# The second cross attention's keys and folded query weights computed at the end of the routed stage before it

## The reference, cut to what matters

```
x = x + tanh(g_ffn[0])   * L0_ffn(layernorm(x))        # 8 experts, top 2 of them for each token
x = x + tanh(g_xattn[1]) * L1_xattn(layernorm(x), ctx, ctx, mask, W_Q, W_K, W_V, W_O)

L1_xattn: Q = x W_Q, K = ctx W_K, V = ctx W_V (16 heads of 64)
          softmax(mask(Q K^T / 8)) V W_O
```

## Time and profile before

| | |
|---|---|
| median of 3 runs | 1459.25 us (1458.04 to 1459.87) |
| the profiled execution: its own time | 1460.75 us |
| its span, first to last instruction | 1458.9 us |
| mean granted TensorE clock | 0.862 of full |
| PE / PEld busy | 1148.7 us (79%) / 793.9 us (54%) |
| DVE / ACT / POOL busy | 708.8 us (49%) / 614.8 us (42%) / 442.1 us (30%) |
| L0f's loop ends on PE | 399.3 us after the span's start |
| L1 opens | 419.1 us |
| L1's first scores | 452.2 us |

### The profile page before, as it was taken

The page is one execution under the profiler, slowest core; times in us unless marked ns, Lnnn a source line. Parts: engine busy times, 40 slices in busy tenths (PEclk is TensorE's granted clock), DMA queues, the critical chain, the costliest instruction groups (busy, mean ns, idle before and its releaser), DMA issues. The chain is left out here.

```text
span 1458.9 us, 26569 instructions
## 1 busy us (share of the span) xinstructions
PE 1148.7 (79%) x8750; PEld 793.9 (54%) x8750; DVE 708.8 (49%) x3304; ACT 614.8 (42%) x1531; POOL 442.1 (30%) x636
## 2 busy tenths in 40 slices
PE   5997875399959999989997874998476999962594
PEld 3675744287725566654444764787352444442473
DVE  3564547133337777634452444111755788755012
ACT  3453442133247776624213230333362666630353
POOL 1673514423403644510000416344010000015343
PEclk8998987599979999999997875699785999975797
DMA  7599120222079940011620011465234222040343
GB/s 198 135 265 226 37 102 28 68 75 83 16 117 120 161 77 2 1 33 44 150 58 15 2 59 41 122 173 137 60 114 126 67 54 68 20 138 18 85 133 91
DMA packets 150263, 128.36 MB, mean 88 GB/s; under 512 B 13205, under 2 KB 126796, under 8 KB 150137
## 3 DMA queue, kind: packets, MB, share of 16 engines
q1 hardware_dynamic: 135256, 107.65, 31.5%
q0 software_dynamic: 7824, 15.32, 4.0%
q10 hardware_dynamic: 7056, 3.81, 1.0%
HBM read 88.89 MB, written 40.85 MB: 89 GB/s over the span
## 5 line engine op out<-in xcount | busy, mean ns | idle before, releaser
L306 POOL TENSOR_TENSOR L_Z<-L_Z,L_mx 128x512 f32<-128x512 f32 x84 | 88.5, 1055 | 276.9 <-DVE L_mx L617 276.9
L2991 DVE CUSTOM_DVE_ANT_0 L3s_masked<-L3s_psS,L3s_trilw 128x512 f32<-128x512 f32 (+3 forms) x256 | 109.0, 487 | 34.8 <-PE L3s_psS L2890 34.3
L908 ACT ACTIVATE L_Z<-L_Z,L_nmx 128x154 f32<-128x154 f32 x256 | 105.1, 414 | 42.3 <-DVE L_nmx L965 42.2
L2962 ACT ACTIVATE L3s_E<-L3s_psT 128x512 f32<-128x512 f32 (+1 forms) x192 | 87.8, 531 | 48.8 <-PE L3s_psT L2903 48.6
L740 POOL TENSOR_TENSOR L_Z<-L_Z,L_rin 128x488 f32<-128x488 f32 x64 | 64.0, 1000 | 125.0 <-DVE L_rin L973 125.0
L617 DVE CUSTOM_DVE_ANT_0 L_Z<-L_psS,L_Z 128x154 f32<-128x154 f32 x256 | 63.4, 313 | 61.1 <-PE L_psS L354 53.6
L808 PE MATMUL L_psS<-L_G,L_xnT 128*128 128x462 f32 x192 | 82.5, 526 | 2.8 <-DVE L_nmx L965 1.4
L965 DVE CUSTOM_DVE_ANT_0 L_Z<-L_psS,L_mask 128x154 f32<-128x154 f32 x256 | 67.7, 313 | 11.4 <-PE L_psS L808 10.9
L515 ACT ACTIVATE L_E<-L_psT 128x512 f32<-128x512 f32 x84 | 46.3, 596 | 56.8 <-PE L_psT L367 56.8
L2890 PE MATMUL L3s_psS<-L3s_KS,L3s_QS 72*128 72x512 bf16 (+3 forms) x256 | 55.3, 333 | 13.0 <-PEq L2876 10.1
L983 DVE COPY L_PT<-L_psT 122x512 f32<-122x512 f32 x64 | 43.6, 682 | 40.5 <-PE L_psT L818 39.7
(11 more groups left out here) (544 smaller groups left out, 2880.7 us busy)
## 6 DMA issues: line engine op xcount, KB each, us to landing
L_Z<-in_fside_Bx16xSxS SPq DMA_DIRECT2D x16, 1232.0 KB
L2f_w<-in_L_ffn_W SPq DMA_DIRECT2D x39, 256.0 KB
slotsL<-empty SPq DMA_DIRECT2D x1, 8320.5 KB, 75.1
L1m_cb<-comb_rows SPq DMA_DIRECT2D x8, 1024.0 KB
L3f_w<-in_L_ffn_fc_w SPq DMA_DIRECT2D x32, 256.0 KB
L0f_w<-in_L_ffn_W SPq DMA_DIRECT2D x24, 256.0 KB
q_parts<-L3s_parts SPq DMA_DIRECT2D x12, 384.0 KB, 5.2
L3s_QS<-q_parts SPq DMA_DIRECT2D x16, 288.0 KB
```

What stands on the lines that cost most here:

```text
L306: nc.gpsimd.tensor_tensor(Z[:, t % NZ, h, 0:KM_], Z[:, t % NZ, h, 0:KM_], top.broadcast_to([P, HG, KM_]), ALU.subtract).then_inc(z_ready, 1)
L908: last = nc.scalar.activation(Z[:, t % 2, h], Z[:, t % 2, h], ACT.Exp, scale=-1.0, bias=nmx[:, t % 2, h:h + 1], accum_out=sums[:, t % 2, h ...
L2962: nc.scalar.activation(E[:, g.par, h, EO[group[0]]:EO[group[0]] + wd], psT[:, k, 0:wd], ACT.Exp).then_inc(t_free, 1)
L2991: last = nc.vector.tensor_tensor_reduce(masked[:, k, at:at + wd], psS[:, k, at:at + wd], trilw[:, S - wd:S], 1.0, LOW, ALU.add, ALU.max, m ...
```

## The change

A new class `Keys1` owns G, which is now allocated around both stages. `Lead0`'s four large tiles are slices of G's memory (`lend`). The keys and G are made at the end of L0f, two heads (one block j) at a time: K^T of a block goes through the two banks of `psT` into a double-buffered KT, its eight products with W_Q through `psA` (a = 0) and `psB` (a = 1) into G. PE does so right after its loop. ACT handles blocks 0 to 3 before its wait for `returned` and the issue of its reads, and one of blocks 4 to 7 ahead of each group that it scales; DVE handles blocks 0 to 3 before its additions, and one of blocks 4 to 7 ahead of each group. L1 loses the keys, the folded weights and their waits and begins with the values.

```diff
 def wide_attention(nc, m, c):
-        G = sb("G", [P, B, H, S2])
+        G = c["G"]
         @block.tensor
-            for j in range(KB): ...   # keys, L749 to L755
             for b in range(B):
                 for j in range(2):
                     n = 2 * b + j
-                    if n < 4:
-                        pe.wait_ge(k_done, 13 + n)
-                    else:
+                    if n >= 4:
                         pe.wait_ge(v_out, n - 3)
             pe.wait_ge(v_out, 2 * B)
-            pe.wait_ge(k_done, 2 * KB)
-            for b in range(B): ...    # folded weights, L774 to L787
             pe.wait_ge(r_out, B)
-            pe.wait_ge(g_out0, G3 * B)
-            pe.wait_ge(g_out1, G3 * B)
         @block.scalar    (L874 to L877 and L884 to L890 removed)
         @block.vector    (L945 to L951 removed)

 class Lead0:
-        self.w1, self.w2, self.b1 = sb("f1", [P, 4 * P]), sb("f2", [P, 4, D]), sb("fb", [P, 4])
-        self.h, self.tmp = sb("fh", [P, 2, 4, 512]), sb("tmp", [P, TB, D])
+        lend = c["keys"].lend
+        self.w1, self.w2, self.b1 = lend([P, 4 * P]), lend([P, 4, D]), sb("fb", [P, 4])
+        self.h, self.tmp = lend([P, 2, 4, 512]), lend([P, TB, D])

+class Keys1:
+    def tensor(self, pe):
+        ctx_all = self.m.ctxT[:].rearrange("p b k -> p (b k)")
+        def keys(j):
+            if j >= 1:
+                pe.wait_ge(self.k_done, 2 * j)
+            for f in range(2):
+                pe.matmul(self.psT[:, f, 0:2 * S2], self.wk[:, j * P:(j + 1) * P], ctx_all[:, f * 2 * S2:(f + 1) * 2 * S2],
+                          start=True, stop=True).then_inc(self.k_full, 1)
+        def scores_weights(j):
+            pe.wait_ge(self.k_done, 2 * j + 2)
+            if j >= 1:
+                pe.wait_ge(self.g_done0, 2 * j)
+                pe.wait_ge(self.g_done1, 2 * j)
+            for f in range(2):
+                for b in range(2):
+                    for a in range(2):
+                        at = (2 * f + b) * S2
+                        last = pe.matmul(self.banks[a][:, f, b * S2:(b + 1) * S2], self.wq[64 * a:64 * a + 64, j],
+                                         self.KT[64 * a:64 * a + 64, j % 2, at:at + S2], start=(b == 0), stop=(b == 1),
+                                         skip_group_check=True)
+                last.then_inc(self.g_full, 1)
+        keys(0)
+        for j in range(self.KB):
+            if j + 1 < self.KB:
+                keys(j + 1)
+            scores_weights(j)
+
+    def scalar(self, act, j):
+        def keep_keys(j):
+            if j >= 2:
+                act.wait_ge(self.g_full, 2 * (j - 1))
+            for f in range(2):
+                act.wait_ge(self.k_full, 2 * j + f + 1)
+                nc.scalar.mul(self.KT[:, j % 2, f * 2 * S2:(f + 1) * 2 * S2], self.psT[:, f, 0:2 * S2], self.SIGN).then_inc(self.k_done, 1)
+        if j == 0:
+            keep_keys(0)
+        if j + 1 < self.KB:
+            keep_keys(j + 1)
+        for f in range(2):
+            act.wait_ge(self.g_full, 2 * j + f + 1)
+            nc.scalar.copy(self.G[:, 2 * f:2 * f + 2, 2 * j], self.banks[0][:, f, 0:2 * S2]...).then_inc(self.g_done0, 1)
+
+    def vector(self, dve, j):     # the same for banks[1], g_done1

 class Collect:
-    def second(self, act):
+    def second(self, act, keys=None):
+        if keys is not None:
+            for j in range(TB):
+                keys.scalar(act, j)
+        for p in range(2):
+            act.wait_ge(self.m.returned[p], 16 * self.m.back[p])
         for g in range(TB):
             act.dma_start(m.XT3[:, g * TB:(g + 1) * TB], self.rows(1, g)).then_inc(self.in1[g], 16)
         act.wait_ge(self.shared, 1)
         for g in range(TB):
+            if keys is not None:
+                keys.scalar(act, TB + g)
             act.wait_ge(self.in1[g], 16)
             ...
-    def add(self, dve):
+    def add(self, dve, keys=None):
         dve.wait_ge(self.shared, 1)
+        if keys is not None:
+            for j in range(TB):
+                keys.vector(dve, j)
         for g in range(TB):
+            if keys is not None:
+                keys.vector(dve, TB + g)
             ...
```

More of the change, by code:

```diff
@@ L748, in _ @@
         def _(pe):
[L749 to L755, removed]
             for b in range(B):
@@ L873, in _ @@
         def _(act):
[L874 to L877, removed]
             act.wait_ge(var_ready, 1)
@@ L883, in _ @@
                 nc.scalar.copy(V[0:KM, b, j * 512:(j + 1) * 512], kv_bank[n % 4][0:KM, :]).then_inc(v_out, 1)
[L884 to L889, removed]
-                                   g_bank[n % 2][:, 0, 0:w * S2].rearrange("p (j k) -> p j k", k=S2)).then_inc(g_out0, 1)
             def turned_x(u):
@@ L1541, in sync @@
     def sync(self, sp):
[L1542 to L1543 removed]
+        for dst, src in ((self.w1, self.c["w1"]), (self.b1[:], self.c["b1"]), (self.w2, self.c["w2"])):
+            sp.dma_start(dst, src).then_inc(self.f_in, 16)
     def gpsimd(self, pool):
@@ L1928, in routed_experts @@
 def routed_experts(nc, m, name, c):
+    keys = c.get("keys")
     J, U, chunks = c["w1"].shape[2] // P, c["U"], c["chunks"]
@@ L1972, in routed_experts @@
         route = lead.route
+        if keys is not None:
+            keys.open(sb, sem, psT, (psA, psB))
         collect = Collect(nc, sem, m, c["key"], route.shared, c.get("out"))
@@ L2043, in _ @@
                 a.end()
-            for p in range(2):
-                act.wait_ge(returned[p], 16 * m.back[p])
-            collect.second(act)
+            collect.second(act, keys)
         @block.tensor
@@ L2106, in _ @@
                 a.end()
+            if keys is not None:
+                keys.tensor(pe)
         @block.vector
@@ L2139, in _ @@
                     n.end()
-            collect.add(dve)
+            collect.add(dve, keys)
         @block.gpsimd
@@ L3051, in stage_list @@
     early.close()
-    routed_experts(nc, m, "L0f", dict(w1=d["L0_ffn_W1"], w3=d["L0_ffn_W3"], w2=d["L0_ffn_W2"], act=ACT.Silu, U=4, chunks=[3, 2],
-                                      key="L0", head=Lead0, lead=dict(kind="L0", E=8, gate=4, wr=w["L0_ffn_Wr"][:], w1=d["L0_xattn_W1"],
-                                                                      b1=d["L0_xattn_b1"], w2=d["L0_xattn_W2"])))
-    if upto == 1: return
-    wide_attention(nc, m, dict(name="L1", gate=1, clear=["L2", "L3"],
-                               wq=w["L1_xattn_W_Q"][:], wk=w["L1_xattn_W_K"][:], wv=w["L1_xattn_W_V"][:],
-                               wo=w["L1_xattn_W_O"][:]))
+    with ExitStack() as own:
+        keys = Keys1(nc, own, m, w["L1_xattn_W_K"][:], w["L1_xattn_W_Q"][:])
+        routed_experts(nc, m, "L0f", dict(w1=d["L0_ffn_W1"], w3=d["L0_ffn_W3"], w2=d["L0_ffn_W2"], act=ACT.Silu, U=4, chunks=[3, 2],
+                                          key="L0", head=Lead0, keys=keys,
+                                          lead=dict(kind="L0", E=8, gate=4, wr=w["L0_ffn_Wr"][:], w1=d["L0_xattn_W1"],
+                                                    b1=d["L0_xattn_b1"], w2=d["L0_xattn_W2"], keys=keys)))
+        if upto == 1: return
+        wide_attention(nc, m, dict(name="L1", gate=1, clear=["L2", "L3"], G=keys.G, wv=w["L1_xattn_W_V"][:],
+                                   wo=w["L1_xattn_W_O"][:]))
     if upto == 2: return
```

43 lines of the change are left out of this document (26 added, 17 removed).

## The result

Four runs of the changed kernel took 1444.57 us in the median (1442.49 to 1445.63), four of the kernel before beside them 1459.56 (1458.04 to 1460.76): a ratio of 0.9902, 95% interval 0.9882 to 0.9922. The profiled execution took 1442.49 us, its span is 1440.5 at a mean granted clock of 0.865. The forecast was 1446.3, in 1443.0 to 1451.5.

What follows compares the result with a forecast made beforehand. L0f's end was taken to wait for its results' HBM round trip, leaving PE a 20 us hole, while PE paced L1's opening. 6.1 us later and 19.0 earlier gave -12.9 of 1459.25: 1446.3, range 1443 to 1451.5.

Steps and rivals of the forecast that it cites:

- Term 1: L0f's end: added key and folded-weight blocks delay ACT's reads and the work behind them, so L1 opens 6.1 us later.
- Start 0.5 after the loop: L0f's end: PE starts the key products 0.5 us after its loop, between bounds 0 and 1.8.
- A block 2.05: L0f's end: two key products and four pairs of folded-weight products take PE 2.05 us a block.
- ACT's reads 11.0 after the loop's end: L0f's end: ACT issues its four reads only after its last copy of block 3, at 410.3 instead of 406.35.
- First scaling 4.6 after the issue: L0f's end: first returned group lands 4.6 us after ACT's issue, bounds 4.5 and 8.2, SP's traffic being mostly through.
- The chain behind it: L0f's end: from the first scaling, ACT's scalings and block copies set the pace; DVE ends at 424.9, L1 opens at 425.2.
- Term 2: L1's opening: without keys and folded weights, first scores come after 14.1 us instead of 33.1, 19.0 us earlier.
- Full clock at the values: L1's opening: the clock stays up through PE's idle time, so term 2 is 21.2; -15.1 us, 1444.2; chance 0.15.
- The second half at half clock: L0f's end: blocks 5 to 7 cost 2.05 us more each, opening 2.2 later; -10.7 us, 1448.6; chance 0.15.
- Late reads: L0f's end: reads land as late as 8.2 us, or PE starts at 1.8; -10 us, 1449.5; chance 0.14.
- The hole is not used: L0f's end: ACT and DVE evict blocks only when results are near; 6.6 us later, -6.3, 1453; chance 0.04.
- no full clock until the attention loop: L0f's end and L1's values: both at half clock, +6.7 us, 1466, chance 0.03; milder form 1458, chance 0.04.

Runs made afterwards that it cites:

- full_rows: Changed kernel with one folded product of all 128 rows per batch instead of two of 64 rows, so G holds other numbers; 1446.11 us, timed once.
- after_again: The changed kernel unedited, timed and profiled a second time; 1440.69 us, ratio 0.9906 to the kernel before.
- after_third: The changed kernel unedited, timed and profiled a third time; 1443.02 us, ratio 0.9908 to the kernel before.
- before: The kernel before the change, in its first profile; median 1459.56 us over four runs.
- before_again: The kernel before the change, unedited, profiled once more; 1453.04 us in one run.
- warm: Changed kernel plus six key products on PE behind block 7 whose results nobody reads; 1444.83 us, timed once.
- sp_tail: Changed kernel with SP issuing all eight reads and blocks 4 to 7 placed after scaling groups, block 7's copies last; 1442.61 us, timed once.
- after: The changed kernel in its first profile; median 1444.57 us over four runs, ratio 0.9902 to the kernel before.
- eight_first: Changed kernel with ACT and DVE handling all eight blocks, instead of four, before ACT's wait and reads; 1447.54 us, timed once.
- sp_reads: Changed kernel with all eight reads issued by SP, none by ACT; 1440.96 us, ratio 0.9922 to the kernel before.

## Why the prediction was right, point by point

The sum came out: -12.9 forecast for the two stretches, -13.2 in the first pair of profiles; 1446.3 forecast, 1444.57 measured, a difference well inside what the untouched parts of the program differ by from execution to execution. The mechanism was right (PE's work fits the hole, ACT's reads come later for it, the opening shrinks to the values at half clock), but that the sum was met to 0.3 us is in part luck: errors in its terms cancel.

**Term 1, the hole, +6.1: measured +6.0** (26.0 against 20.0; 5.2 to 6.5 over the other pairs of profiles). Its steps:
- Start 0.5 after the loop, between bounds 0 and 1.8: measured 0. PE ran into code it had not executed without a gap. One stall of 0.70 in block 1 of the first profile, put down to issue, is the only thing like the 1.79 of the earlier trace rows, and it didn't return in the two others.
- A block 2.05: measured 2.48. The step that failed is the unit price. The earlier trace rows gave me the price of folded products among themselves (0.253 a pair), and of keys among themselves; the kernel before changed between the two kinds once, the new one does it thirteen times. full_rows puts 0.4 us on a change there and back.
- ACT's reads 11.0 after the loop's end: measured 12.5, 11.7 and 11.7 in the three profiles.
- First scaling 4.6 after the issue: 3.4 without any wait, 4.5 and 3.4 in the three profiles; 3.0 to 5.2 in the edited ones. The reason given, that SP's reads are mostly through, is not borne out: the 3.0 is the case long behind SP's reads and the 5.2 the one closest behind them, but after_again and after_third, issued 3.6 and 3.7 behind SP's, differ by 1.1 or more, and before and before_again, issued together with SP's, took 4.6 and 4.2. What sets the landing stays open.
- The chain behind it: I had ACT setting the pace from the first scaling to L1, 10.3. It is 9.7 to the last addition and 0.3 on top, and DVE sets it, back to back at 2.54 a group. The end that I put down, 424.9, is also 0.5 later than its own terms behind ACT's end give (423.5, a crossing of 0.2, an addition of 0.69).

Blocks 1.7 dearer, a start 0.5 cheaper, a tail 0.3 shorter and landings up to 1.2 shorter made the total right.

**Term 2, the opening, 14.1: measured 13.9, 14.2, 14.1.** Half clock at the values' start was right. Its two terms cancel in part: at full clock the opening takes 11.4 (forecast 11.9), and half clock costs 2.4 to 2.8 (forecast 2.2). The table load ran at 415.38, during the statistics, as I had let it. PE's waits in the opening name ACT's copies of the values and of the turned tokens, never G or the square root.

**The rivals.** *Full clock at the values*: not in the changed kernel; warm shows that case, and it is worth 2.4 to 2.8, not 2.2. *The second half at half clock*: no. PE worked in bursts with idle times of 0.62 and 0.95 us between them from 404 to 412, and the granted clock stayed at 1.00 throughout, as it did in full_rows across an idle time of 1.76; the rule of the Trainium skill's page TensorE: Matmul & The Clock Gate, section Why this matters for your kernels, that gaps between bursts bring the clock down, did not bite at these gaps, and did at the longer one ahead of L1. *Late reads*: in full_rows, where they cost 0.6 beyond my 4.6, not in the changed kernel. *The hole is not used* and *no full clock until the attention loop*: no sign of either.

## What to carry to other kernels

A wait for a round trip through HBM can hide work of another stage, but the end moves if its evictions stand on the queue that issues the reads: here the reads go out 11.7 to 12.5 us after the loop instead of 7.2, and DVE's last addition follows 9.7 us after the first scaling. Let an engine without other duties issue them, and place the hidden work so that only its last copies stand behind the last product: the two together took 2.7 us off the hole (26.2 in after_again, 23.5 in sp_tail, one profile each), too little to show in single times. When work is cut into small pieces of two shapes, price the change between the shapes, not the shapes alone; and ahead of dense matmuls, a few products that nobody reads can be cheaper than restarting at 1.2 GHz, if they end before the other engines do: two took 1.6 us off the opening for 0.4 of hole.

## What the hardware showed that I had not expected

- Changing between matmuls on 128 rows and on 64 rows costs PE about 0.4 us there and back, 0.3 of it on the way to 64 rows: 2.48 to 2.49 us for a block with both changes, 2.08 to 2.09 without, at the same columns in sequence.
- The clock does not fall at a fixed distance from the last matmul. PE's last product ended at 412.24 in after, and the clock was down within 413 to 414; in eight_first it ended at 415.92, and the clock was down within 418 to 419 (0.90); in sp_reads PE paused from about 415.2 to 418.4, started the values at 1.00, and the clock fell a microsecond into them (0.68 in 419 to 420, with PE busy for all of it). Nor does the length of the last pause decide: in sp_tail PE paused for 1.40 only, and the clock fell just behind the pause (0.69 in 417 to 418); in full_rows it stayed at 1.00 across an idle time of 1.76 between two blocks. What decides stays open.
- Parts of the program that no edit touched differ by up to 8 us between executions of the same code or of kernels alike there (178.6 to 186.5 up to the end of L0's attention), while the two stretches under study repeat within about one.
